# A decoder layer in 16 chunks on one core: new hand-written step orders, a PSUM ring dealt by use, and the weights loaded in two groups

## The chip, the cores and the metric

One Trainium2 chip, of which one core is used. The metric is the device time of one execution in microseconds (us), the median of several runs. Abbreviations: PE is TensorE (PEld its weight loads), DVE is VectorE, ACT is ScalarE, POOL is GpSimd, SP is SyncE, which here only issues DMAs.

## The reference, cut to what matters

All is float32. `x` is 128 sequences of 64 tokens of width 128; `ctx` has the same shape.

```python
# 1. a Mamba block
proj = rms_norm(x) * norm_scale @ in_w + in_b            # 128 -> 512
hidden, gate = split(proj)                               # 256 each
conv = silu(causal_conv4(hidden) + conv_b)
ts, B, C = split(conv @ xproj_w)                         # 64, 16, 16
delta = softplus(ts @ dt_w + dt_b)
for t: state = exp(A * delta) * state + delta * B * conv # 256 channels x 16 states
       y = sum_n(state * C) + D * conv
x = layernorm(x + (y * silu(gate)) @ out_w + out_b)
# 2. cross attention, 16 heads of 8, keys and values from ctx
x = layernorm(x + attention(x, ctx))
# 3. experts: 8 of width 176, top 2 by a router, and one shared
x = layernorm(x + sum_e cw[e] * (silu(x @ wg[e]) * (x @ wu[e])) @ wd[e] + shared(x))
```

## The kernel before, in words

**Chunks and stages.** The batch is cut into 16 chunks of 8 sequences, 512 tokens (`T`). A chunk goes through five stages: *head* (load of x, RMS norm, transposes), *front* (input projections, convolution, B, C, delta), *scan* (16 states, one after the other), *back* (last sums of the scan, output projection, first layer norm, attention, second layer norm, router, start of the experts) and *tail* (rest of the experts, down projection, third layer norm, output).

**Turns.** The program is a sequence of 20 turns, t = -2 to 17. In turn t each engine walks once through a list of its own, `ORDER[engine]`, made from `ORDER_TEXT`. An entry such as `back.up_u3` is a step: stage, name, index. It works on chunk t + `CHUNK_OF[stage]`, with head 2, front 1, scan 0, back -1, tail -2, and is left out where that chunk doesn't exist. So turns 2 to 14 hold all five stages, the first four lack the later stages and the last three lack the earlier ones; all of them use the same lists. Every engine runs its list strictly in order and waits on semaphores inside the steps. A list is a cycle: what stands at its end is followed by what stands at its start, on the next turn.

**Steps that matter below**, on PE unless said otherwise:
- `B_row n` (L478) spreads B of state n over the partitions; DVE `drive n` (L871) multiplies it in PSUM, DVE `scan n` (L881) is the recurrence over [128, 1024]. `B_row n+1` waits for `scan n`, as they share a bank. ACT `decay k` (L630) makes the factors, POOL `prod n` (L1009, and L1014 where two states are joined) multiplies by C, `y_sum k` (L496) adds the product up in PSUM.
- `x1T`, `x2T` (L544) transpose the result of a layer norm. A layer norm is: PE fills a bank (`mout`, `aout`, `down`), DVE `stats` (L855), POOL `stats` (L1027 to L1034), ACT `norm` (L784), which also frees the bank.
- `score`, DVE `score` (maximum, L928), ACT `exp` (8 activations, L760), DVE `sum`, POOL `scale` (L1059), `turn` (L568), ACT `turn` (L769), `mix` (L576), ACT `mix` (L775): attention, eight times per chunk. `aout1` (L582) waits for the last ACT `mix`.
- `up_g i`, `up_u i` (L592), 13 each: gate and up projections of the experts. ACT `up_g` (tanh, L799) and DVE `up_g` (L978) consume a gate bank, DVE `up_u` (L983) or, for i in `ON_POOL`, ACT `up_u` (L807) an up bank. POOL `gu` (L1071) and `cw` (L1080) multiply; the weights of `cw` come over DRAM: PE and ACT `cwT`, SP `cw_out`, SP `cw_in`, two slots. `down` (L608) needs all of them; its first matmul waits for `cw9`, a later one for `cw10`.
- ACT `dt` (L706), `soft` (L712), `soft_ln` (L716, a table load ahead of it and one behind it, ahead of the next tanh or exp), then DVE `delta` (L909, L912): softplus. ACT `squares` (L642) waits for `delta`, since both use `sp_a`.
- POOL `k`, ACT `km`: masked keys. They overwrite what `down` reads and so wait for the last `down1`.

**The ring.** 20 kinds of PE steps (`IN_RING`), 75 steps a turn, write into four PSUM banks. `ring_place` gives a step its bank: the position of the step in the list, modulo 4. A step waits until the bank's user before it has been freed by its consumer (`ring_free`). As 75 is 3 modulo 4, the distance to the user before is 4 steps, but 3 steps for some of the first steps of a turn, and in turns with stages left out the positions that are skipped leave their banks unused.

**The opening.** SP issues 17 weight DMAs (L415), all on the semaphore `weights_in`, and then `x_in` of chunk 0 (L422). PE, ACT, DVE and POOL each wait for all 17. DVE clears `decay`, `hpad`, `vm` and others ahead of that wait and makes 10 more constants behind it, the last but two of them `wu` times 0.5 (L843); PE, ACT and POOL wait for all (`consts_v` at `CONSTS` = 11) before their first step.

Of the kernel before, what the change touches and what calls it, by code (L numbers as in the profile page):

```python
# [73 lines left out]

ORDER_TEXT = {
# [1093 lines left out]
```

## Time and profile before

| | us |
|---|---|
| median of 3 runs | 1959.86 (1947.79 to 1962.64) |
| the profiled execution | 1953.28 |
| its span, first to last instruction | 1951.5 |
| PE busy in it | 1698.4 (87%) |
| POOL busy | 1539.2 (79%) |
| DVE busy | 1508.2 (77%) |
| ACT busy | 1407.5 (72%) |

The 1.8 us between span and time lie before the first and behind the last instruction. A "busy" PE is not one at its peak: its clock is granted at one of two levels, and the same matmul takes twice as long at the lower. Idle time of an engine matters only where the chain that sets the time runs through it.

### The profile page before, as it was taken

How to read it: one execution, taken by the hardware profiler on the slowest of the kernel's cores; microseconds unless marked ns; L12 is line 12 of the kernel's file. 1: busy time of each engine (PE TensorE's matmuls, PEld its weight loads, DVE VectorE, ACT ScalarE, POOL GpSimd, SP SyncE). 2: the span in 40 equal slices, each digit the busy share in tenths (PEclk: the TensorE clock that was granted, in tenths of full speed). 3: DMA queues.
4: the chain of work that ended last, by engine and by line, in shares of the span. 5: the costliest groups of instructions: out<-in, count | busy, mean ns of one | idle time of the engine just before them, and what ended most of it. 6: DMA issues, size and time to landing. Idle time of an engine off the chain costs nothing. (4 is left out here: it accounts for less than half of the span.)

```text
span 1951.5 us, 25799 instructions
## 1 busy us (share of the span) xinstructions
PE 1698.4 (87%) x7138; PEld 975.5 (50%) x7138; DVE 1508.2 (77%) x1891; ACT 1407.5 (72%) x4370; POOL 1539.2 (79%) x1284
## 2 busy tenths in 40 slices
PE   3477898989989899998989999898999989898977
PEld 1124464654646465464646546464655636455644
DVE  3878887887878888788878888788888878878422
ACT  3558778696877968697786869778686967857362
POOL 0457888887878888888888888888888878888735
PEclk8678999999989999999999999899999989999989
DMA  4112131232213223222212322131222312131202
GB/s 123 48 44 66 61 92 54 72 88 85 73 55 88 66 70 88 87 74 74 85 51 68 87 87 83 60 83 60 76 77 87 82 60 77 61 87 60 71 6 65
DMA packets 125918, 140.50 MB, mean 72 GB/s; under 512 B 44048, under 2 KB 69456, under 8 KB 125776
## 3 DMA queue, kind: packets, MB, share of 16 engines
q1 hardware_dynamic: 125776, 138.86, 23.9%
q8 instruction: 58, 0.95, 0.2%
q14 instruction: 84, 0.69, 0.1%
HBM read 133.84 MB, written 4.98 MB: 71 GB/s over the span
## 5 line engine op out<-in xcount | busy, mean ns | idle before, releaser
L1009 POOL TENSOR_TENSOR prod<-state,c_rep 128x1024 f32<-128x1024 f32 x256 | 605.9, 2370 | 43.8 <-DVE state L881 24.0
L881 DVE TENSOR_TENSOR_SCAN state<-decay,p_drive 128x1024 f32<-128x1024 f32 x256 | 583.8, 2280 | 26.8 <-ACT decay L630 14.8
L496 PE MATMUL p_y<-prod,ident 128*128 128x512 f32 x768 | 403.6, 619 | 2.2 <-POOL prod L1014 1.6
L630 ACT ACTIVATE decay<-delta,a_neg 128x504 f32<-128x504 f32 x512 | 361.7, 726 | 60.3 <-DVE state L881 57.1
L871 DVE TENSOR_TENSOR p_drive<-u,p_drive 128x1024 f32<-128x1024 f32 x256 | 312.1, 1219 | 44.1 <-PE p_drive L478 43.6
L760 ACT ACTIVATE ex<-p_ring,nmax 128x64 f32<-128x64 f32 x1024 | 307.8, 355 | 5.4 <-DVE nmax L928 3.1
L592 PE MATMUL p_ring<-x2T,wu 128*128 128x512 f32 x416 | 216.6, 610 | 43.6 <-DVE kT L978 41.9
L592 PE MATMUL p_ring<-x2T,wg 128*128 128x512 f32 x416 | 233.3, 653 | 17.5 <-DVE km L978 10.6
L760 ACT ACTIVATION_READ_ACCUMULATOR ex<-p_ring,nmax 128x1 f32 x1024 | 247.3, 250 | 0.0
L799 ACT ACTIVATE gt<-p_ring 128x512 f32<-128x512 f32 x208 | 123.5, 595 | 102.8 <-PE p_ring L592 102.1
L496 PEld LDWEIGHTS p_y<-prod,ident 128*128 128x128 f32 x768 | 139.7, 197 | 109.5 <-issue 93.9
L1059 POOL TENSOR_TENSOR ex<-ex,rden 128x512 f32<-128x512 f32 x128 | 139.7, 1092 | 65.3 <-DVE rden L932 58.8
L1080 POOL TENSOR_TENSOR km<-km,cwr 128x512 f32<-128x512 f32 x128 | 175.7, 1377 | 8.7 <-DMA cwr<-cw_rows 8.2
L1071 POOL TENSOR_TENSOR km<-km,us 128x512 f32<-128x512 f32 x80 | 115.3, 1442 | 64.3 <-ACT us L807 64.1
L563 PE MATMUL p_ring<-km,qs 128*128 128x512 f32 x256 | 135.7, 613 | 24.0 <-POOL km L1053 18.3
L1014 POOL TENSOR_TENSOR prod<-prod 128x1024 f32<-128x1024 f32 x64 | 150.9, 2357 | 5.0
L592 PEld LDWEIGHTS p_ring<-x2T,wu 128*128 128x128 f32 x416 | 76.9, 194 | 152.9 <-issue 73.1
L576 PEld LDWEIGHTS p_ring<-exT,vm 128*128 128x128 f32 x1024 | 128.9, 191 | 41.0 <-issue 28.7
L592 PEld LDWEIGHTS p_ring<-x2T,wg 128*128 128x128 f32 x416 | 80.4, 205 | 123.6 <-issue 92.1
L576 PE MATMUL p_ring<-exT,vm 128*128 128x128 f32 x1024 | 138.2, 278 | 4.1 <-ACT exT L769 2.2
L784 ACT ACTIVATE x<-p_ring,shift,rstd 128x128 f32<-128x128 f32 x192 | 77.3, 453 | 84.6 <-POOL shift L1034 84.0
L855 DVE BATCH_NORM_STATS2 stats<-p_ring 128x6 f32<-128x128 f32 x192 | 47.1, 287 | 112.7 <-PE p_ring L608 83.9
(138 smaller groups left out, 3171.9 us busy)
## 6 DMA issues: line engine op xcount, KB each, us to landing
c_rep<-c_rows SPq DMA_DIRECT2D x256, 256.0 KB, 3.6
cwr<-cw_rows SPq DMA_DIRECT2D x64, 256.0 KB, 3.2
ctxT<-in_ctx_t SPq DMA_DIRECT2D x32, 256.0 KB, 4.2
cwr<-cw_rows SPq DMA_DIRECT2D x32, 224.0 KB, 2.7
...
```

The costliest lines, as they stand in the source:

```text
L496: pe.matmul(p_y[1 - first][:], ident[:], prod[:, slot_of(c, n), 1 - first, :], start=False, stop=n == STATE - 1).then_inc(prod_used.sem, 1)
L563: mm = pe.matmul(p[:], qs[:, i, :, :].rearrange("p s q -> p (s q)"), km[:, i, :, :].rearrange("p a k -> p (a k)"), start=True, stop=True)
L576: mm = pe.matmul(p[:, 0:128], vm[:, i, q, :], exT[:, q, :], start=q == 0, stop=q == QUADS - 1)
L592: mm = pe.matmul(p[:], (wg if name == "up_g" else wu)[:, i, :], x2T[:], start=True, stop=True)
L630: act.activation(decay[:, n % 2, j, :].rearrange("p (b t) -> p b t", t=SEQ)[:, :, 1:], delta[:, c.parity, j, :].rearrange("p (b t) -> p b ...
L760: e = act.activation(ex[:, i % 2, a, :], p[:, a * SEQ:(a + 1) * SEQ], ACT.Exp, bias=nmax[:, i % 2, a:a + 1], accum_out=den[:, i % 2, a:a + 1])
L871: dve.tensor_tensor(p_drive[:], u[:, c.parity, :, :], p_b.unsqueeze(1).to_broadcast([128, HALVES, T]), ALU.mult).then_inc(drive_ready.sem, 1)
L881: dve.tensor_tensor_scan(state[:, slot_of(c, n), :, :].rearrange("p j t -> p (j t)"), decay[:, n % 2, :, :].rearrange("p j t -> p (j t)"), ...
L1009: pool.tensor_tensor(mine, state[:, slot_of(c, n), :, :], c_rep[:, n % C_SLOTS, :].unsqueeze(1).to_broadcast([128, HALVES, T]), ALU.mult). ...
L1014: pool.tensor_tensor(mine, mine, prod[:, slot_of(c, n - 1), :, :], ALU.add).then_inc(join_ready.sem, 1)
L1059: pool.tensor_tensor(ex[:, i % 2, :, :], ex[:, i % 2, :, :], by_group(rden[:, i % 2, :]).to_broadcast([128, PAIRS, SEQ]), ALU.mult).then_i ...
L1080: pool.tensor_tensor(acts[i], acts[i], cwr[:, slot, :], ALU.mult).then_inc(act_ready.sem, 1)
```

## The change

1. **Three sets of lists.** `FIRST_TEXT` serves turns -2 to 1, `ORDER_TEXT` (new) turns 2 to 14, `LAST_TEXT` turns 15 to 17. All lists hold the same steps as before, but for the place of the cut between two turns: some steps that opened a turn now close the turn before it (on PE 14 steps from `tail.up_g6` to `y_sum29`, now `back.up_g6` and so on; on DVE `drive14` and `scan14`; on POOL `cw7` to `cw9` and `gu10`).
2. **The ring is dealt by use.** The steps that really run, over all turns, get banks 0, 1, 2, 3, 0, ... in turn: the distance is always 4.
3. **Weights in two groups**, behind the first x. `x_in` of chunk 0 comes first, then 9 loads that head and front need (`weights_in`), then 8 others (`weights_late`). PE waits for the late ones at the first `xp`, POOL at the first `add_out_b`, DVE at the first `taps` of chunk 1, where it also scales `wu` (`half_wu`; the first `up_u0` waits for that). ACT and POOL start when only `eps` is there; ACT waits for all constants at its first `hid`. The clearing of `decay`, `vm`, `r_sel`, `r_cw` moves behind the constants on DVE.

```diff
-RING = [step for step in ORDER["pe"] if step[1] in IN_RING]
+USES = [use for t in TURNS for use in steps_at("pe", t) if use[0] in IN_RING]
+PLACE = {use: (k % BANKS, k // BANKS) for k, use in enumerate(USES)}
...
+LAST_FIRST, FIRST_LAST = 1, CHUNKS - 1
+def steps_at(engine, t):
+    part = "first" if t <= LAST_FIRST else "last" if t >= FIRST_LAST else "main"
...
-            for to, src in ((vecs[:], vec), (win[:], w_in), (ident[:], c_ident), (wxp[:], w_xproj),
...
+            sp.dma_start(xf[:], x[bass.ds(0, T), :].rearrange("(g p) d -> p g d", p=128)).then_inc(x_in.sem, 16)
+            for to, src in ((vecs[:], vec), (ident[:], c_ident), (win[:], w_in), (masks[:], c_masks),
+                            (wattn[:], w_attn), (rowb[:, 0, :], rows[0].partition_broadcast(128)),
+                            (rowb[:, 1, :], rows[1].partition_broadcast(128)), (sel_bc32, c_sel_bc),
+                            (less32, c_less)):
                 sp.dma_start(to, src).then_inc(weights_in.sem, 16)
+            for to, src in ((wxp[:], w_xproj), (wdt[:], w_dt), (wout[:], w_out), (wrt[:], w_router),
+                            (tri[:], c_tri), (wg[:], w_gate), (wu[:], w_up), (wd[:], w_down)):
+                sp.dma_start(to, src).then_inc(weights_late.sem, 16)
```

The lists for turns 2 to 14 where the prediction follows them, from the last sums of attention to the first steps that the next turn opened with before ("|" is the cut between two turns):

```
PE before:   back.mix7 back.aout1 scan.y_sum18 back.x2T0 scan.B_row12 back.x2T1 scan.y_sum19 back.route0
             scan.B_row13 front.dt0 back.up_g0 back.up_g1 front.dt1 back.up_u0 back.up_g2 back.up_u1
             scan.y_sum22 scan.B_row14 back.cwT0 back.up_g3 back.up_u2 back.up_g4 front.gate1 back.up_u3
             scan.y_sum23 scan.y_sum26 back.up_u4 scan.B_row15 back.up_g5 back.up_u5 | tail.up_g6
PE after:    back.x2T0 back.mix7 scan.y_sum15 back.aout1 scan.B_row12 front.dt0 scan.y_sum18 scan.y_sum19
             back.x2T1 scan.B_row13 back.route0 front.dt1 back.up_g0 back.up_g1 back.up_g2 scan.B_row14
             scan.y_sum22 back.up_u0 back.up_u1 back.cwT0 back.up_u2 back.up_g3 front.gate1 back.up_g4
             scan.y_sum23 back.up_u3 back.up_u4 scan.y_sum26 scan.B_row15 back.up_g5 back.up_u5 back.up_g6
ACT before:  front.dt0 back.up_g0 back.up_g1 front.dt1 scan.decay29 back.up_g2 front.soft0 scan.decay30
             back.up_u1 back.cwT0 front.soft_ln0 back.up_u2 scan.decay31 back.up_g3 front.gate1 back.up_g4
             head.squares0
ACT after:   front.dt0 back.r_exp0 back.up_g0 scan.decay28 back.up_g1 front.dt1 scan.decay29 back.up_g2
             back.up_u1 scan.decay30 scan.decay31 back.cwT0 front.soft0 back.up_u2 back.up_g3
             front.soft_ln0 back.up_g4 front.gate1 back.up_u4 head.squares0
DVE before:  back.route0 scan.drive13 back.r_rank0 back.up_g0 back.up_g1 scan.scan13 back.r_cw0
             back.up_g2 back.up_u0 | back.drive14 back.scan14 tail.up_g3 scan.delta0 tail.up_u3 tail.up_g4
DVE after:   scan.drive13 back.route0 scan.scan13 back.r_rank0 back.up_g0 back.up_g1 back.r_cw0
             back.up_g2 back.up_u0 scan.drive14 scan.scan14 | tail.up_g3 scan.delta0 tail.up_g4 tail.up_u3
```

Elsewhere in these lists: PE runs `v1`, `B_row4`, `q0`, `y_d0`, `y_d1` between `down1` and `score0` (before: `B_row4`, `q0`, `y_d0`, `v1`); ACT runs `front.tanh1` between `exp3` and `exp4` (before: between `exp1` and `exp2`); DVE runs `drive6` behind `score3` (before: ahead of it); POOL runs `prod12` ahead of `r_rank0` (before: behind it).

## Rows read from the trace of the kernel before

**Rows 1.** Six stretches: busy us by engine (instructions), granted PE clock, DMA share, GB/s.
```profile
0.00:50.40 50.40, 18.55 (x25) 6.27 (x25) 14.81 (x28) 18.78 (x37) 1.20 (x5) 0.83 0.41 123
50.40:129.20 78.80, 46.97 (x78) 16.46 (x78) 65.18 (x43) 39.13 (x69) 45.87 (x20) 0.65 0.16 51
129.20:228.90 99.70, 76.82 (x294) 41.14 (x294) 83.79 (x97) 81.56 (x259) 71.13 (x56) 0.90 0.17 51
228.90:1703.70 1474.80, 1349.67 (x5798) 783.68 (x5798) 1215.09 (x1522) 1138.12 (x3550) 1255.38 (x1041) 0.97 0.25 75
1703.70:1817.70 114.00, 102.06 (x439) 60.11 (x440) 90.12 (x114) 72.18 (x240) 98.27 (x84) 0.97 0.25 77
1817.70:1951.50 133.80, 104.30 (x505) 67.80 (x503) 39.18 (x94) 57.75 (x219) 67.37 (x81) 0.92 0.14 42
```
**Rows 2.** Waits of PE's matmuls, turns 2 to 14: total us, times, longest.
```profile
PE p_ring L592 <- DVE kT L978: 36.4, 13, 3.5
PE p_ring L544 <- ACT x L784: 25.8, 13, 2.0
...
PE p_ring L582 <- ACT aT L775: 8.2, 13, 0.6
```
**Rows 3.** Timeline of PE in one turn: start, us, instructions [idle before <-releaser].
```profile
1001.11 0.41 PE L544 MATMUL p_ring<-ident,x 128*128 128x128 f32 x2 [1.98 <-ACT x L784]
...
1017.51 1.02 PE L592 MATMUL p_ring<-x2T,wg 128*128 128x512 f32 x2
1018.37 1.02 PE L522 MATMUL p_ring<-xnT,win 128*128 128x512 f32 x2
1022.40 1.33 PE L592 MATMUL p_ring<-x2T,wu 128*128 128x512 f32 x2 [3.01 <-DVE kT L978]
```
**Rows 4.** The granted clock around those waits.
```profile
1002.70:1009.50 6.80, 6.80 (x12) 2.37 (x11) 3.58 (x10) 3.14 (x6) 5.01 (x4) 0.50 0.01 2
1023.20:1026.60 3.40, 3.40 (x5) 1.35 (x4) 3.36 (x4) 1.89 (x9) 3.40 (x2) 0.50 0.34 116
```
**Rows 5.** Timeline of ACT between the same two waits.
```profile
1010.71 0.69 ACT L706 ACTIVATE delta<-p_ring,vecs 128x512 f32<-128x512 f32 x1 [0.46 <-PE p_ring L530]
...
1015.85 1.28 ACT L716 ACT_TABLE_LOAD   x1
1017.14 1.06 ACT L716 ACTIVATE sp_a<-sp_a 128x1024 f32<-128x1024 f32 x1
...
1018.71 1.28 ACT L630 ACT_TABLE_LOAD   x1
...
1020.62 0.58 ACT L799 ACTIVATE gt<-p_ring 128x512 f32<-128x512 f32 x1
```
**Rows 6.** Timeline of DVE there.
```profile
1021.66 0.69 DVE L978 SCALAR_TENSOR_TENSOR kT<-gt,p_ring 128x512 f32<-128x512 f32 x1 [2.51 <-ACT gt L799]
1022.26 1.44 DVE L909 TENSOR_TENSOR delta<-delta,sp_a 128x1024 f32<-128x1024 f32 x1
1023.74 2.17 DVE L912 TENSOR_TENSOR u<-delta,h 128x1024 f32<-128x1024 f32 x1
```
**Rows 7.** POOL's longest wait in turns 2 to 14.
```profile
POOL km L1071 <- ACT us L807: 56.5, 13, 7.5
```
**Rows 8.** Groups of POOL in turns 2 to 14: busy us, mean ns of one.
```profile
L1009 POOL TENSOR_TENSOR prod<-state,c_rep 128x1024 f32<-128x1024 f32 x208 | 491.5, 2366 | 13.2 <-DVE state L881 7.9 <-issue 5.0
...
L1080 POOL TENSOR_TENSOR km<-km,cwr 128x512 f32<-128x512 f32 x105 | 145.6, 1392 | 1.6 <-DMA cwr<-cw_rows 1.3
```
**Rows 9.** Timeline of the opening.
```profile
16.04 0.23 ACT L618 ACTIVATE a_neg<-vecs 128x32 f32<-128x32 f32 x1 [14.04 <-DMA rowb<-in_rows]
18.33 0.31 ACT L642 ACTIVATE sp_a<-xf 128x128 f32<-128x128 f32 x1 [2.06 <-DVE a_neg L847]
26.34 0.69 ACT L666 ACTIVATE hpad<-p_ring,vecs 128x512 f32<-128x512 f32 x1 [2.17 <-PE p_ring L522]
```
**Rows 10.** DMA issues of the first 20 us: KB each, us to landing.
```profile
zc<-in_c_less SPq DMA_DIRECT2D x1, 128.0 KB, 2.5
```

More of the change, by code:

```diff
@@ L69 @@
 CHUNK_OF = {"head": 2, "front": 1, "scan": 0, "back": -1, "tail": -2}
+FIRST_TEXT = {
[17 rows of a table added]
+    "act": (
[15 rows of a table added]
+    "dve": (
[12 rows of a table added]
+    "pool": (
[12 rows of a table added]
+}
 ORDER_TEXT = {
     "pe": (
[16 rows of a table removed]
-    "act": (
[15 rows of a table removed]
-    "dve": (
[12 rows of a table removed]
-    "pool": (
[12 rows of a table removed]
[16 rows of a table added]
+    "act": (
[15 rows of a table added]
+    "dve": (
[12 rows of a table added]
+    "pool": (
[12 rows of a table added]
+}
+LAST_TEXT = {
[17 rows of a table added]
+    "act": (
[15 rows of a table added]
+    "dve": (
[12 rows of a table added]
+    "pool": (
[12 rows of a table added]
 }
@@ L142, in read_step @@
     return stage, bare, int(name[len(bare):])
-ORDER = {engine: [read_step(word) for word in text.split()] for engine, text in ORDER_TEXT.items()}
+TEXTS = {"first": FIRST_TEXT, "main": ORDER_TEXT, "last": LAST_TEXT}
+ORDER = {part: {engine: [read_step(word) for word in text.split()] for engine, text in texts.items()}
+         for part, texts in TEXTS.items()}
+TURNS = range(-max(CHUNK_OF.values()), CHUNKS - min(CHUNK_OF.values()))
+LAST_FIRST, FIRST_LAST = 1, CHUNKS - 1
+def steps_at(engine, t):
+    part = "first" if t <= LAST_FIRST else "last" if t >= FIRST_LAST else "main"
+    return [(name, i, t + CHUNK_OF[stage]) for stage, name, i in ORDER[part][engine]
+            if 0 <= t + CHUNK_OF[stage] < CHUNKS]
 IN_RING = ("down", "mout", "k", "xnT", "v", "hid", "x1T", "q", "score", "mix", "turn", "aout",
            "xp", "gate", "x2T", "route", "up_g", "up_u", "cwT", "dt")
-RING = [step for step in ORDER["pe"] if step[1] in IN_RING]
-STAGE_OF = {step[1:]: step[0] for step in RING}
-assert len(STAGE_OF) == len(RING)
+USES = [use for t in TURNS for use in steps_at("pe", t) if use[0] in IN_RING]
+PLACE = {use: (k % BANKS, k // BANKS) for k, use in enumerate(USES)}
+assert len(PLACE) == len(USES)
 class Signal:
@@ L200, in ring_place @@
 def ring_place(name, i, m):
-    stage = STAGE_OF[name, i]
-    at = RING.index((stage, name, i))
-    bank = at % BANKS
-    same = [j for j in range(bank, len(RING), BANKS)]
-    t = m - CHUNK_OF[stage]
-    before = 0
-    for j in same:
-        chunk = t + CHUNK_OF[RING[j][0]]
-        before += min(max(chunk, 0), CHUNKS) + (j < at and 0 <= chunk < CHUNKS)
-    return bank, before
+    return PLACE[name, i, m]
 def build(nc, x, ctx_t, vec, rows, w_in, w_xproj, w_dt, w_out, w_attn, w_router, w_gate, w_up, w_down,
@@ L397, in turns @@
         def turns(engine, step):
-            for t in range(-max(CHUNK_OF.values()), CHUNKS - min(CHUNK_OF.values())):
-                for stage, name, i in ORDER[engine]:
-                    if 0 <= t + CHUNK_OF[stage] < CHUNKS:
-                        step(name, i, Chunk(t + CHUNK_OF[stage]))
+            for t in TURNS:
+                for name, i, m in steps_at(engine, t):
+                    step(name, i, Chunk(m))
         block = stack.enter_context(nc.Block())
@@ L591, in step @@
                 elif name in ("up_g", "up_u"):
+                    if name == "up_u" and c.m == 0 and i == 0:
+                        pe.wait_ge(half_wu.sem, 1)
                     mm = pe.matmul(p[:], (wg if name == "up_g" else wu)[:, i, :], x2T[:],
@@ L660, in step @@
                     act.activation(xnT[:, i * 256:(i + 1) * 256], p[:, 0:256], ACT.Copy,
-                                   scale=column(V_NORM)).then_inc(free(name, i), 1)
+                                   scale=column(V_NORM)).then_inc(free(name, i, c.m), 1)
                 elif name == "hid":
+                    if c.m == 0 and i == 0:
+                        act.wait_ge(consts_v.sem, CONSTS)
                     p = filled(act, name, i, c.m)
@@ L666, in step @@
                     act.activation(hpad[:, i, :, TAPS - 1:], p[:].rearrange("p (b t) -> p b t", t=SEQ),
-                                   ACT.Identity, bias=column(V_INB + i)).then_inc(free(name, i), 1)
+                                   ACT.Identity, bias=column(V_INB + i)).then_inc(free(name, i, c.m), 1)
                 elif name == "tap":
@@ L769, in step @@
                     act.activation(exT[:].rearrange("p a q -> p (a q)"), p[:],
-                                   ACT.Copy).then_inc(free(name, i), 1)
+                                   ACT.Copy).then_inc(free(name, i, c.m), 1)
                 elif name == "mix":
@@ L785, in step @@
                                            scale=rstd[:, ln, g:g + 1], bias=shift[:, ln, g:g + 1])
-                    a.then_inc(free(LN_IN[ln], half), 1)
+                    a.then_inc(free(LN_IN[ln], half, c.m), 1)
                 elif name == "x2T":
                     p = filled(act, name, i, c.m)
-                    act.activation(x2T[:, i * 256:(i + 1) * 256], p[:, 0:256], ACT.Copy).then_inc(free(name, i), 1)
+                    act.activation(x2T[:, i * 256:(i + 1) * 256], p[:, 0:256], ACT.Copy).then_inc(free(name, i, c.m), 1)
                 elif name == "r_exp":
@@ L806, in step @@
                         act.wait_ge(gu_ready.sem, gu_ready.at(c.m - 1, len(ON_POOL) - 2 + k))
-                    act.activation(us[:, k % 2, :], p[:], ACT.Copy).then_inc(free(name, i), 1)
+                    act.activation(us[:, k % 2, :], p[:], ACT.Copy).then_inc(free(name, i, c.m), 1)
                 elif name == "cwT":
@@ L811, in step @@
                         act.wait_ge(cw_out.sem, cw_out.at(c.m - 1))
-                    act.activation(cwT[:], p[0:EXPERTS, :], ACT.Copy).then_inc(free(name, i), 1)
+                    act.activation(cwT[:], p[0:EXPERTS, :], ACT.Copy).then_inc(free(name, i, c.m), 1)
                 elif name == "decay":
@@ L888, in step @@
                 if name == "taps":
+                    if c.m == 1 and i == 0:
+                        dve.wait_ge(weights_late.sem, 16 * n_late)
+                        dve.tensor_scalar(wu[:], wu[:], 0.5, None, ALU.mult).then_inc(half_wu.sem, 1)
                     j, pair = divmod(i, 2)
```

76 lines of the change are left out of this document (38 added, 38 removed), and 220 rows, old and new, of tables (FIRST_TEXT, LAST_TEXT, ORDER_TEXT).

## The prediction

> **What bounds the kernel now.** I read the stretches first. Turns 2 to 14 take 1474.8 of 1951.5 us, 113.4 us each [rows 1]. In them PE is busy 1349.67 us (91.5%), POOL 1255.38 (85%), DVE 82%, ACT 77% [rows 1]. So PE is nearest to being the bound, and what it loses is the first thing to look at: 1474.8 - 1349.67 = 125 us, 9.6 us a turn. The list of its waits names the two largest: a matmul of L592 behind DVE's `kT` (36.4 us, 13 times, 2.8 a turn) and one of L544 behind ACT's norm (25.8 us, 2.0 a turn) [rows 2]. In the timeline these are `up_u3`, which waits 3.0 us for a bank, and `x2T1`, 2.0 us [rows 3]. Each wait is followed by a second loss: right after them the granted clock is 0.50 (1.2 instead of 2.4 GHz) for 6.8 and for 3.4 us [rows 4]. Over all 13 turns the clock is 0.97 [rows 1], so 6% of the time is spent at half rate, 6.8 us a turn, and half of that, 3.4 us, is lost although it counts as busy.
>
> Is PE on the path that sets the time? Followed back from the wait at 1022.40: it is ended by DVE `up_g3` at 1021.66 [rows 6], that by ACT `up_g3` at 1020.62 [rows 5]. ACT ran without a pause from `dt1` at 1010.71 on, with `soft_ln` and its two table loads (1.28 + 1.06 + 1.28 = 3.6 us) in between [rows 5]. `dt1` waited for PE, which came there at half rate from `x2T1` at 1001.11 [rows 3, 4]. `x2T1` waited for the second layer norm. So the loop runs through x2T1, the expert projections, the down projection, attention and the next x2T1, partly on PE and partly on ACT and POOL. The other end stretches are not of that kind: in the first 50.4 us PE is busy 18.55 and DVE 14.81 us, and in the last 133.8 us PE is busy 78%, POOL 50% and the others less [rows 1]. They are bound by latency.
>
> **The opening.** Before, everyone waits for 17 loads: ACT's first operation is at 16.04, and the squares of x start at 18.33, after the constants [rows 9]. After, x and 9 loads (1.1 MB of the 4.1) go first. SP spends some 0.45 us on an issue and 1.3 on the pair for `rowb`; the tenth is issued at about 5.6 us. A load that isn't behind the three large ones lands in 2.5 us (`less` [rows 10]). So the early group is there at 8.1 to 8.5, and ACT starts the squares at about 8.5: 9.8 us sooner. Two covers have to hold. ACT's first `hid` (before at 26.34, after at 16.5 [rows 9]) now waits for constants and for the clears moved behind them: 1.6 us of constants and about 6.6 of clears behind 8.3 end at 16.5, just hidden; if a us late, it costs that us. The first `xp`, a convolution behind that `hid`, waits for the late group, whose bytes are all in by 16 to 17 as before [rows 9]. Value -9.8, between -10.5 and -7.
>
> The Trainium skill ("DMA: Bandwidth & Descriptors", Queues, rings and completion order) states that each of the DMA engines consumes its descriptors in ring order, but that completion is not in order of issue: a small load's semaphore says nothing of an older one on other engines. That speaks for waiting for a count over all nine, as the change does; by it the group is ready at its slowest load. The trace agrees as to the ring order: the small `rowb`, issued last, is what ended the common wait at 16.04 [rows 9].
>
> **Turns 0 and 1** take 78.8 and 99.7 us at clocks of 0.65 and 0.90 [rows 1]. In turn 0 only the scan with front and head run, and its chain B_row, drive, scan can't be shortened: 16 times about 4.4 us is 70. Own lists (no stage that is absent shapes them) can take at most 8 us there; the scaling of `wu` adds 1 us of DVE in turn 0. Value -2.5 for turn 0 and -1.5 for turn 1, together -4, between -12 and +3.
>
> **Turns 2 to 14, wait by wait.** A PE step of 512 columns starts every 0.86 us at full rate [rows 3].
> - `x2T1` (2.0 us). Between `aout1`, which starts its layer norm, and it stood 1.3 us of other PE work; now `dt0`, `y_sum18`, `y_sum19` stand there too, 2.8 us. The latency stays. 1.5 us go.
> - `aout1` (8.2 / 13 = 0.6 us [rows 2]) has `y_sum15` ahead of it now. 0.6 goes, and 0.3 at `aout0` in the same way.
> - `up_u3` (2.8 us). Its bank's user before was `up_g3`, freed by DVE after ACT. Now 4 uses before is `up_u2`, freed by ACT, and `up_g3`'s bank goes to `up_u4`. I count from `x2T1` = 0. PE: `up_g3` starts at 10.4, `up_u4` could at 14.7. ACT, now with `soft_ln` and its loads behind `up_g3` and without waiting for `dt1` at half rate, ends `up_g3` at about 13.7 (before: 20.1 [rows 3, 5]); DVE at 14.6. The 2.8 us go.
> - What comes in their place: `gate1` and `up_g4` are behind `soft_ln` on ACT: 13.7 + 1.28 + 1.06 + 1.28 + 0.6 + 0.7 = 18.6 [rows 5]. `up_g5` takes `gate1`'s bank and could start at 16.7: a new wait of 1.9 us. On DVE `delta0` now has to wait for `soft_ln` at 16.0 and takes 1.44 + 2.17 [rows 6]; `up_g4` follows and frees its bank at 20.3, where `up_u5` could have started at 19.5: 0.8 us. Against these stands the wait of 0.7 that `up_g5` had before. Added 2.0.
> - `score0` waits 1.1 us for POOL's keys. It has 0.9 us more work ahead of it (`y_d1`), but `score1` takes the bank of `down1`, and the norm that frees it comes no sooner: it moves, 0 gained. The wait at `turn0` stays. `drive6` behind `score3` gives ACT its maximum 1.2 us sooner, but ACT is nearly full there, and `tanh1` (0.6) now lies between `exp3` and `turn4`: 0.6 added.
> - POOL: `up_u1` reaches it some 5 us sooner, so its longest wait (4.3 us a turn [rows 7]) shrinks to 2, but then `cw0` waits about 1.3 for its DMA. From `gu1` at 9.5 POOL has up to the end of `cw9` 17 `gu` and `cw` of 1.27 to 1.39 us, `prod13` to `prod15` with a join, 4 x 2.37 [rows 8], and a power of 1.0: 32 to 34 us, with that DMA 43 to 45. PE wants `down0` at 45 by its own work. For a wait of POOL on ACT in between I add 1.0.
> - Clock: the two long waits that the half-rate stretches follow are gone or spread out; I take half of the 3.4 us back, 1.7.
>
> Sum: -(1.5 + 0.9 + 2.8 + 1.7) + (2.0 + 0.6 + 1.0) = -3.3 us a turn, 110.1 us; times 13, -43. Bounds: all of the waits named and all of the clock, nothing added, -8.5; nothing gained and the added waits in full, +3.5.
>
> The ring dealt by use matters little by itself here: the distance was already 4 for all but the first steps of a turn. Dealing costs no instruction. SP's list issues `C13` ahead of `C11` and `C12`, so both wait for `prod9`; they are needed after a join, `prod10` and `stats3`, 6 us later, and land in about 4. Nothing.
>
> **Turn 15 and the end.** Turn 15 has no front, yet takes 114.0 us like the others [rows 1]; POOL is busy 98.27 of them. Its waits are those above, so I take -3.3. In the last 133.8 us the chain is: POOL's `cw` of chunk 14, the down projection, keys, eight rounds of attention, router, projections, `cw` again, `down`. Each step waits for the one before, and the order of independent ones changes little: -1.7. Together -5, between -15 and +4.
>
> **Sum.** -9.8 - 4 - 43 - 5 = -62. The profiled execution took 1953.28 us (span 1951.5), so it would be 1891.5. The median of the three runs is 6.6 us above the profiled one; the same saving from there gives 1898. I take 1895.
>
> **Rivals.**
> 1. *The clock comes back whole.* With no PE wait of 2 us left, the half-rate stretches end, and small waits no longer add up to one: 3.4 instead of 1.7, and a turn without slow stretches reaches `dt1` and `up_u1` sooner, so half of the 3.6 added goes as well. -6.8 a turn, -88: 1953.3 - 88 - 19 = 1846, say 1850. For it: every stretch in rows 4 follows a wait. Against it: the new waits at `up_g5` and `up_u5`. The skill ("TensorE: Matmul & The Clock Gate", A second HAM failure mode: psum-queue depth-cycling) says that micro-idles between groups of matmuls, by cycling through PSUM banks, are enough to make the clock swing. By that rule some of the 3.4 us stays lost; the trace shows falls after waits of 2 and 3 us and can't tell for smaller ones.
> 2. *POOL takes PE's place.* It has 96.6 us of work a turn [rows 1]. If only `gu1`'s wait shrinks and 1.3 us of DMA and 2 us at `gu1` remain, POOL gains 1.1 us a turn: -14 - 19 = -33, 1920. POOL would then be over 87% busy and `down0` would wait for `cw9`.
> 3. *The loop doesn't get shorter*: what goes at `up_u3` comes back at `up_g5`, `up_u5` in full. Then only opening and ends count: -19, 1934 to 1941.
> 4. *Slower.* One mechanism: ACT's queue. `up_g3` stands behind `cwT0`, and that behind the router, whose `r_rank` now follows `scan13` (2.3 us) on DVE. If ACT gets to `cwT0` 5 us later than I count, `up_g3`, `soft_ln`, `gate1`, `delta` and `up_g4` all are 5 us late, PE waits that much more at `up_u4` or `up_g5`, and the clock falls (1.7 more): -3.3 + 5 + 1.7 = +3.4 a turn, +44 - 19 = +25, 1978. It decides from 3.3 us of such delay on for a turn, from about 5 for the whole. Against it: the router has 2 us of spare time in my count.
>
> **How the numbers follow.** Forecast 0.52, rival 1 0.14, rival 2 0.18, rival 3 0.10, rival 4 0.06. The range, 1850 to 1937, reaches from rival 1 to rival 3 and leaves out about 2 in 10. About 1% (20 us) is what a measurement can tell from no change. Faster by over 1%: forecast, rivals 1 and 2, part of 3: 0.86. Within 1%: most of 3: 0.08. Slower: 0.06.
>
> **What would show it.** Squares of x at 8 to 9 us; `hid` at 16 to 17; turns of 109 to 111 us between two `delta`; no wait over 1 us at `x2T1` and `up_u3`, one of about 2 at `up_g5`; clock about 0.98; POOL 87 to 88% busy in turns 2 to 14; the end from the last scan about 130 us. A turn of 113 with new waits on PE would refute the main term, a `hid` at 18 the cover in the opening.

## The result, and the profile after

The kernel after took 1910.16 us (median of 4 runs, 1905.50 to 1915.23), the kernel before beside it 1961.25. The ratio is 0.976, with a 95% interval of 0.973 to 0.979: 2.4% faster. The profiled execution took 1910.89 us, its span is 1909.1 against 1951.5. 1895 had been forecast, 1850 to 1937 as the range. One execution among all those below, the profiled one of t4_drive6, ran about twice as long as the others of its kernel (3382.5 us), and none of its rows is used.

The six stretches of the kernel after (cut at the starts of DVE's `delta0` of chunks 0, 1, 2 and 15 and at the end of its last `gated1`, as in [rows 1]; us, busy us of PE, weight loads, DVE, ACT and POOL, granted clock, DMA share, GB/s):

```profile
0.00:40.20 40.20, 18.51 (x25) 6.26 (x25) 13.99 (x27) 18.59 (x37) 1.20 (x5) 0.79 0.38 122
40.20:114.30 74.10, 44.91 (x75) 15.66 (x76) 65.68 (x44) 38.37 (x68) 45.80 (x20) 0.70 0.23 68
114.30:208.50 94.20, 78.06 (x294) 41.48 (x299) 81.48 (x97) 80.84 (x258) 71.12 (x56) 0.95 0.17 50
208.50:1662.40 1453.90, 1335.90 (x5709) 772.28 (x5800) 1250.56 (x1522) 1129.39 (x3550) 1246.05 (x1041) 0.99 0.25 77
1662.40:1790.50 128.10, 118.65 (x475) 67.02 (x480) 99.10 (x127) 79.92 (x253) 113.96 (x96) 0.97 0.26 82
1790.50:1909.10 118.60, 88.44 (x458) 62.00 (x458) 28.91 (x80) 51.65 (x208) 51.40 (x70) 0.86 0.10 33
```

Set against [rows 1], with the forecast in brackets: opening 50.4 to 40.2, -10.2 (-9.8); turns 0 and 1, 178.5 to 168.3, -10.2 (-4); turns 2 to 14, 113.4 to 111.8 us each, -20.9 in all (-43); turn 15 and the end together, 247.8 to 246.7, -1.1 (-5; the last two stretches only trade 14 us, since the last lists let the scan run later). The sum is -42.4 (-62). So two thirds of the forecast gain came, and what is missing is missing in the main turns. DVE got busier there by 35.5 us although it has the same 1522 instructions [rows 1]; that turned out to be the trail.

PE's busy time in the fourth row is not to be set against [rows 1]: 90 of its matmul records are missing there, all of them of `B_row`, about half of those that ran. Behind a missing record PE looks idle for some 0.3 us longer than it was.

The opening, timeline of ACT (start, us, instruction, idle before and its releaser), answers to [rows 9]:

```profile
8.07 0.23 ACT L754 ACTIVATE a_neg<-vecs 128x32 f32<-128x32 f32 x1 [6.07 <-DMA zc<-in_c_less]
8.21 0.29 ACT L778 ACTIVATE sp_a<-xf 128x128 f32<-128x128 f32 x1
...
16.39 0.69 ACT L804 ACTIVATE hpad<-p_ring,vecs 128x512 f32<-128x512 f32 x1 [2.42 <-DVE r_cw L985]
```

The squares start at 8.21 where 18.33 stood. The first `hid` is at 16.39 and waits for DVE's clears (`r_cw`): that cover is used up, as counted.

The waits of turns 2 to 14 (total us, times, longest) answer to [rows 2, 7]:

```profile
POOL acts_more L1223 <- DMA cwr<-cw_rows: 34.5, 26, 2.9
POOL km L1214 <- ACT us L945: 30.5, 13, 4.2
...
PE p_ring L678 <- ACT x L922: 18.4, 26, 1.0
...
PE p_ring L660 <- DVE h L1041: 13.7, 13, 1.1
...
PE p_ring L728 <- ACT gh L823: 11.8, 12, 1.1
...
PE p_ring L697 <- ACT x L922: 11.0, 13, 0.9
```

`up_u3`'s 2.8 us a turn and `aout1`'s 0.6 are gone, `x2T1` waits 0.45 instead of 2.0 (L678 is `x1T1` and `x2T1` together). POOL's longest wait fell from 4.3 to 2.3 us a turn [rows 7], but its waits for `cwr` rows are now 34.5 us (12.7 before). And PE has new ones: 1.05 us at `front.xp0`, behind DVE's `silu1` (L660), and 0.9 at `up_g5` (L728). Summed up, PE stands idle 9.1 us a turn (1453.90 less 1335.90, over 13), somewhat less for the missing records, where it was 9.6. So the lists took every long wait away and little of the waiting time.

PE where the loop closes, turn 8, answers to [rows 3], and the clock behind it to [rows 4] (PE alone):

```profile
968.84 1.13 PE L710 MATMUL p_ring<-exT,vm 128*128 128x128 f32 x8 [0.40 <-ACT exT L907]
972.24 1.12 PE L664 MATMUL p_ring<-xp_sb,wdt 64*128 64x512 f32 x2 [0.51 <-DVE state L1018]
975.71 0.41 PE L678 MATMUL p_ring<-ident,x 128*128 128x128 f32 x2 [0.43 <-ACT x L922]
...
995.25 1.12 PE L728 MATMUL p_ring<-x2T,wg 128*128 128x512 f32 x2 [1.15 <-ACT gh L823]
996.86 1.12 PE L728 MATMUL p_ring<-x2T,wu 128*128 128x512 f32 x2 [0.49 <-DVE km L1118]
```
```profile
978.90:982.30 3.40, 3.40 (x5) 0.50 0.00 0
```

Half-rate time in turns 2 to 14 fell from 95.6 us to 34.1. Where it is left, it begins 2.2 to 3.7 us behind the start of `x2T1`. The 0.51 ahead of `dt0` in these rows is no wait of `dt0`: the record of `B_row12` is missing there. In s3_drive6_again (below) it is present, and the same place reads

```profile
1064.96 0.39 PE L609 MATMUL p_drive<-xp,sel_bc 128*128 128x512 bf16 x1 [0.19 <-DVE state L1018]
1065.28 1.12 PE L664 MATMUL p_ring<-xp_sb,wdt 64*128 64x512 f32 x2
```

So what stands ahead of the fall is 0.40 at `mix7`, about 0.2 at `B_row12`, 0.43 at `x2T1` and 0.19 at `route0`, and the longest wait before these is `xp0`'s 1.05, 28 us ahead. In s1_d6only (below), where `xp0` doesn't wait, the clock still fell in three turns, one of them at 970.4 us, with no wait over 0.43 in the 30 us before. Rows 3 and 4 had shown it after waits of 2 and 3 us only, and the prediction left open whether it falls without one: it does. That agrees with what the Trainium skill says on micro-idles between groups of matmuls ("TensorE: Matmul & The Clock Gate", A second HAM failure mode: psum-queue depth-cycling). But these small waits don't decide it. They stand at the same places, equal to 0.02 us, in three of the four turns without any half-rate time (in the fourth two of them are longer), and in s3, where no turn has any. What decides stays open.

### The profile page after: what moved, and what is told of

The parts are those of the page before. It is cut to its first block and busy times, and to the rows that moved or that the text cites. A ratio compares the mean times of both kernels' runs of the same rounds, so it can differ in the third digit from the quotient of the medians.

```text
span 1909.1 us, 25699 instructions
## 1 busy us (share of the span) xinstructions
PE 1684.5 (88%) x7035; PEld 964.7 (51%) x7138; DVE 1539.7 (81%) x1891; ACT 1398.8 (73%) x4370; POOL 1529.5 (80%) x1284
## 5 line engine op out<-in xcount | busy, mean ns | idle before, releaser
L627 PE MATMUL p_y<-prod,ident 128*128 128x512 f32 x768 | 391.4, 609 | 10.2 <-POOL prod L1149 5.7
L898 ACT ACTIVATION_READ_ACCUMULATOR ex<-p_ring,nmax 128x1 f32 x1024 | 255.4, 262 | 0.0
L728 PE MATMUL p_ring<-x2T,wg 128*128 128x512 f32 x416 | 226.8, 650 | 13.2 <-ACT gh L823 12.3
L1202 POOL TENSOR_TENSOR ex<-ex,rden 128x512 f32<-128x512 f32 x128 | 144.2, 1127 | 94.1 <-DVE rden L1072 94.1
L728 PE MATMUL p_ring<-x2T,wu 128*128 128x512 f32 x416 | 208.9, 603 | 7.5 <-DVE km L1118 6.5
L1223 POOL TENSOR_TENSOR km<-km,cwr 128x512 f32<-128x512 f32 x128 | 179.6, 1413 | 21.5 <-DMA cwr<-cw_rows 20.3
L697 PE MATMUL p_ring<-km,qs 128*128 128x512 f32 x256 | 135.4, 622 | 25.6 <-ACT x L922 12.7
L728 PEld LDWEIGHTS p_ring<-x2T,wg 128*128 128x128 f32 x416 | 82.3, 205 | 126.2 <-issue 82.9
L710 PEld LDWEIGHTS p_ring<-exT,vm 128*128 128x128 f32 x1024 | 125.0, 191 | 33.1 <-issue 12.0
L744 PE MATMUL p_ring<-wd,km 128*128 128x128 f32 x1024 | 127.9, 279 | 6.9 <-POOL acts_more L1223 6.8
L1214 POOL TENSOR_TENSOR km<-km,us 128x512 f32<-128x512 f32 x80 | 102.6, 1285 | 38.4 <-ACT us L945 37.0
```

The lines of the kernel that those rows point to most:

```text
L627: pe.matmul(p_y[1 - first][:], ident[:], prod[:, slot_of(c, n), 1 - first, :], start=False, stop=n == STATE - 1).then_inc(prod_used.sem, 1)
L710: mm = pe.matmul(p[:, 0:128], vm[:, i, q, :], exT[:, q, :], start=q == 0, stop=q == QUADS - 1)
L728: mm = pe.matmul(p[:], (wg if name == "up_g" else wu)[:, i, :], x2T[:], start=True, stop=True)
L744: mm = pe.matmul(p[:, g * D:(g + 1) * D], acts[j][:, (2 * i + g) * 128:(2 * i + g + 1) * 128], wd[:, j, :], start=False, stop=j == FFN_TIL ...
L898: e = act.activation(ex[:, i % 2, a, :], p[:, a * SEQ:(a + 1) * SEQ], ACT.Exp, bias=nmax[:, i % 2, a:a + 1], accum_out=den[:, i % 2, a:a + 1])
L1202: pool.tensor_tensor(ex[:, i % 2, :, :], ex[:, i % 2, :, :], by_group(rden[:, i % 2, :]).to_broadcast([128, PAIRS, SEQ]), ALU.mult).then_i ...
```

## The experiments

**The change in four parts.** Three kernels build it up from the opening, a fourth leaves out its last lists.

```
# l1_open: opening as changed; before's lists in all turns; before's ring (bank = place in the list % BANKS)
# l2_ring: l1_open with the ring dealt by use
# l3_main: the kernel after with
TEXTS = {"first": ORDER_TEXT, "main": ORDER_TEXT, "last": ORDER_TEXT}
# l4_first: the kernel after with
TEXTS = {"first": FIRST_TEXT, "main": ORDER_TEXT, "last": ORDER_TEXT}
```

> The kernel before with nothing but the opening of the change: x first, weights in two groups, clears behind the constants. Lists and ring as before. Theory 'the opening is carried through': the first delta comes at 40 instead of 50 us, every later turn keeps its length, 10 us less in all, ratio 0.995. Rival 'given back': turn 0 is bound by what it was anyway (the scaling of wu, 1 us, and weights that come late), so that turns 0 and 1 grow by 3 or more and under 7 us are left.

> The kernel above with the ring dealt by use as well; lists still those of before, in all turns. Theory 'the ring by itself does nothing': turns 2 to 14 stay at 113.4 us within 0.3, since the distance was 4 for all but the first few steps of a turn; under 4 us in all. Rival 'the ring is the gain': up_u3 no longer meets up_g3's bank in some turns (as 75 is 3 modulo 4 the dealing shifts the bank but not the distance, so it would have to come from the steps with distance 3), turns shorter by 1 us or more, 13 us in all.

> The change without FIRST_TEXT and LAST_TEXT: the new ORDER_TEXT in all 20 turns. Theory 'each list counts in its own turns': turns 2 to 14 at 111.8 us as in the changed kernel (-1.6 each, -21 in all against the kernel above), turns 0 and 1 near 79 and 100, the whole about 12 us above the changed kernel. Rival 'the new main list does it everywhere': turns 0 and 1 at 74 and 94 already, the whole within 4 us of the changed kernel.

> The change without LAST_TEXT alone: FIRST_TEXT in turns -2 to 1, ORDER_TEXT from 2 on. Theory 'the end is bound by latency, not by order': within 3 us of the changed kernel. Rival 'the last list matters': turn 15 or the end is longer by 5 us or more.

Measured, as ratios to the kernel before: opening 0.994 (0.992 to 0.997), with the ring 0.994 (0.991 to 0.997), with the new main list everywhere 0.986 (0.982 to 0.990), with the first lists too 0.978 (0.974 to 0.982), all 0.976. So the ring by use shows no worth of its own within these intervals, and the other parts add up, but for the last lists, whose share (0.978 to 0.976) the times can't tell from nothing. l3_main lies 17 us above the kernel after where 12 were expected. Row of turns 2 to 14 of l1_open, then turn 0, turn 1 and all from the last `delta0` on of l3_main, then of l4_first:

```profile
218.50:1695.20 1476.70, 1347.94 (x5798) 784.25 (x5798) 1208.66 (x1523) 1139.26 (x3550) 1262.80 (x1041) 0.97 0.25 75
```
```profile
40.30:123.50 83.20, 44.42 (x76) 15.64 (x76) 68.41 (x43) 39.61 (x70) 46.45 (x20) 0.67 0.22 60
123.50:221.90 98.40, 81.33 (x303) 43.26 (x302) 83.72 (x96) 78.19 (x256) 71.62 (x56) 0.93 0.18 49
1675.90:1927.30 251.40, 204.52 (x937) 128.37 (x937) 128.85 (x206) 132.44 (x461) 165.91 (x165) 0.93 0.19 59
```
```profile
38.10:113.80 75.70, 43.62 (x76) 15.32 (x76) 65.87 (x44) 39.16 (x68) 45.58 (x20) 0.70 0.21 66
113.80:207.30 93.50, 78.88 (x299) 41.62 (x299) 81.43 (x96) 80.09 (x258) 71.16 (x56) 0.94 0.18 51
1657.60:1908.10 250.50, 205.08 (x937) 127.77 (x937) 127.50 (x206) 131.99 (x461) 166.20 (x165) 0.94 0.19 59
```

A main turn is 113.6 us with the old list (l1_open) and 111.9 with the new one (l3_main). The new main list is bad in turns 0 and 1 (181.6 us against 178.5 before); the first lists repair that and more (169.2). By the traces the main list also costs some 3 us at the end (250.5 and 251.4 against 247.8), and the last lists win just that back: their gain of about 4 is against the new main list, 1 against the kernel before.

**What bounds the main turns now?** Two kernels take work off POOL and off PE. A third gives the `cwr` rows a third buffer.

```
# t1_pool_less, in POOL's cw
-  pool.tensor_tensor(acts[i], acts[i], cwr[:, slot, :], ALU.mult
+  w = 8 if i in (4, 5) else T
+  pool.tensor_tensor(acts[i][:, 0:w], acts[i][:, 0:w], cwr[:, slot, 0:w], ALU.mult
# t2_pe_less, in PE's y_sum
+  w = 64 if n == 14 else T
+  pe.matmul(p_y[1 - first][:, 0:w], ident[:], prod[:, slot_of(c, n), 1 - first, 0:w], ...
# t3_slots3
-  CW_SLOTS = 2
+  CW_SLOTS = 3
+  cw_slot = [cwr[:, 0, :], cwr[:, 1, :], aT[:]]
```

> The changed kernel, with cw4 and cw5 multiplied over 8 of 512 columns only (leaves out most of the routing weights of these two expert tiles): 2.4 us less of POOL work a turn, between gu1 and cw10. Theory 'POOL bounds the stretch from x2T1 to down1' (61.4 us now, of it 38.3 from gu1 to the end of cw10): turns 2 to 14 fall by 1.5 to 2.4 us from 111.8. Rival 'PE bounds it': no change within 0.4 us.

> The changed kernel, with y_sum28 and y_sum29 over 64 of 512 columns only (leaves out most of state 14 in the sum): 1.5 us less of PE work a turn, in the same stretch from x2T1 to down1. Theory POOL: no change within 0.4 us, PE waits for cw9 or x1T1 instead. Rival PE: turns shorter by 1.2 to 1.5 us, perhaps more by the clock.

> The changed kernel with three slots for the routing weights instead of two (the third is aT, which is idle then): cw_in for cw i no longer waits for cw i-2 but for cw i-3. Theory 'POOL with its DMA waits bounds the stretch': the 3.1 us a turn that POOL waits for cwr (cw8 1.84, cw10 0.74, cw0 0.51) fall to under 1, turns shorter by 1 to 2.5 us, 15 to 35 us in all, which would beat the changed kernel. Rival: the stretch is bound by PE's own work behind it, or SP's queue delays the loads as well: under 0.4 us a turn.

t1 took 1888.1 us (ratio 0.968, 0.960 to 0.976): by the ratios 0.9% less than the kernel after. Its profile shows 1.6 us a turn, of which 1.0 remains between turns without half-rate time (109.6 against 110.6). t2 took 1905.55 (0.977, 0.969 to 0.985), no measurable gain. So PE's own work no longer bounds, and POOL's does in part: rival 2 is half right. t3 didn't do what was expected. POOL's waits for `cwr` rows fell from 44.8 us to 6.3 and POOL ends `cw10` 4.6 us sooner after `x2T1`, yet it took 1916.94 (0.982, 0.976 to 0.989), by the ratios 0.6% more than the kernel after. The two intervals overlap; the traces agree with the times (a main turn is 112.6 us where it was 111.8). The down projection ends 0.7 us later after `x2T1` than in the kernel after: `mout1`, ahead of it on PE, now waits for DVE's `up_u12`.

```profile
PE p_ring L670 <- DVE acts_more L1124: 26.9, 12, 2.3
```

That wait is no second path by the order of the work. The step ahead of `up_u12` on DVE, `gated_h0`, got longer. Its group in turns 2 to 14, in the kernel after and in t3 (busy us, mean ns of one):

```profile
L1045 DVE SCALAR_TENSOR_TENSOR gate<-gate,gh 128x512 f32<-128x512 f32 x26 | 17.8, 683 | 0.0
```
```profile
L1046 DVE SCALAR_TENSOR_TENSOR gate<-gate,gh 128x512 f32<-128x512 f32 x26 | 66.9, 2572 | 0.0
```

In twelve of the thirteen turns `gated_h0` takes 4.8 us instead of 0.7. In t3 POOL's row of `gu` and `cw` has no gap left, and DVE's operation ends when that row does (795.71 to 798.21 are two `cw`):

```profile
793.97 4.78 DVE L1046 SCALAR_TENSOR_TENSOR gate<-gate,gh 128x512 f32<-128x512 f32 x1
```
```profile
794.49 1.27 POOL L1215 TENSOR_TENSOR acts_more<-acts_more,us 128x512 f32<-128x512 f32 x1
795.71 2.50 POOL L1224 TENSOR_TENSOR acts_more<-acts_more,cwr 128x512 f32<-128x512 f32 x2
```

In the remaining one, turn 5 (from 547.1 us on), `gated_h0` takes 1.15, `mout1` doesn't wait, and the turn is 109.15 us long, where turns of the kernel after without half-rate time take 110.2 to 110.9. So where DVE's operation was not held, the third slot went with a turn shorter by over 1 us, as expected; in the other twelve turns the hold cost more than that. That is one turn of one trace; no kernel moved `gated_h0` out of the way.

**Where the main turns lost what they won.** I cut a turn in four legs by the starts and ends of PE's steps (means over chunks 3 to 12, us):

```
                      before   after   s1      s2      s3      s4
x2T1 to end of down1   65.42   61.44   60.86   61.51   60.21   60.67
down1 to score1         6.45    6.29    6.29    6.29    6.29    6.29
score1 to aout0        27.72   29.46   28.20   29.47   28.13   28.13
aout0 to x2T1          13.90   14.64   14.64   14.64   14.62   14.12
```

The first leg won 4.0 us, the attention legs gave 2.5 back (half-rate time lies in the first leg). I suspected the place of `drive6` and `scan6` behind `sum2`, which waits for ACT's `exp2`. t4_drive6 and s3_drive6_again are one kernel, and s1 and s2 are its two halves. One edit in VectorE's main list:

```
 after  "front.silu0 back.score3 back.sum2 scan.drive6 scan.scan6 back.score4 scan.drive7 back.sum3 "
 t4, s3 "front.silu0 scan.drive6 back.score3 back.sum2 scan.scan6 back.score4 back.sum3 scan.drive7 "
 s1     "front.silu0 scan.drive6 back.score3 back.sum2 scan.scan6 back.score4 scan.drive7 back.sum3 "
 s2     "front.silu0 back.score3 back.sum2 scan.drive6 scan.scan6 back.score4 back.sum3 scan.drive7 "
```

> The changed kernel with one local order of DVE put back in the main list: drive6 ahead of score3 and sum2, sum3 ahead of drive7, as it was before. Theory 'DVE's chain of scans in the attention stretch was lengthened by putting drive6 behind sum2, which waits for ACT' (score1 to aout0 29.5 us against 27.7 before): that stretch falls by 0.5 to 1.5 us, turns to about 111. Rival 'the stretch is longer for PE's or ACT's order (tanh1, front.xp0 waiting 1.1 us)': no change or longer.

> The kernel after, and in VectorE's main list only scan.drive6 moved ahead of score3 and sum2 (drive7 stays ahead of sum3). In the kernel after, drive6 and scan6 stand behind sum2, which waits for ScalarE's exp2, so the scan chain stands still for that wait and the later scores of the attention leg come late. Theory (it is this wait that lengthened score1 to aout0 from 27.7 to 29.5 us): that leg is about 28 us, a turn without half-clock stretches about 109.3 us, and the time about 1893 us, some 17 below the kernel after. Rival (it was the order of sum3 and drive7): nothing, 1910 us.

> The kernel after, and in VectorE's main list only sum3 set ahead of drive7 (drive6 stays behind sum2). Theory of drive6's wait: score1 to aout0 stays within 0.3 us of 29.5 and the time is 1905 to 1912 us. Rival: sum3 is what releases ScalarE's scaling of group 3 and TensorE's mix3, so this alone gives the gain: the leg about 28 us and about 1893 us.

> The kernel with both moves in VectorE's main list (the one of t4_drive6) once more, for its trace. Theory: score1 to aout0 about 28 us against 29.5 of the kernel after, turns without half-clock stretches about 109 us against 110.6, half-clock time in turns 2 to 14 no more than the 34 us of the kernel after, span about 1888 us. Rival (the leg is as it was, and the gain is the clock's): half-clock time near 0, turns still 110.5 us.

t4 took 1888.29 us (0.967, 0.961 to 0.974). s3 took 1887.29 (0.966, 0.960 to 0.972), s1 1885.34 (0.964, 0.959 to 0.969), s2 1907.30 (0.975, 0.970 to 0.980). So moving `drive6` alone gives 1.3%, the other half nothing, and the leg is 28.2 us as expected. The leg's 1.26 us a turn are 16 of the 24 us; most of the rest is half-rate time, 13.7 us in turns 2 to 14 of s1 against 34.1. The expected number came, but not for the expected reason. DVE from `drive6` to `silu1` in the kernel after, where `score1` started at 931.64, and POOL beside it:

```profile
940.06 1.21 DVE L1008 TENSOR_TENSOR p_drive<-u,p_drive 128x1024 f32<-128x1024 f32 x1
...
944.94 1.23 DVE L1008 TENSOR_TENSOR p_drive<-u,p_drive 128x1024 f32<-128x1024 f32 x1 [0.71 <-remote]
...
948.46 2.60 DVE L1041 SCALAR_TENSOR_TENSOR h<-h,zc 128x512 f32<-128x512 f32 x1
```
```profile
940.29 1.04 POOL L1202 TENSOR_TENSOR ex<-ex,rden 128x512 f32<-128x512 f32 x1 [0.29 <-DVE rden L1072]
...
947.14 1.05 POOL L1202 TENSOR_TENSOR ex<-ex,rden 128x512 f32<-128x512 f32 x1
948.14 2.37 POOL L1149 TENSOR_TENSOR prod<-state,c_rep 128x1024 f32<-128x1024 f32 x1
```

And the same in s1_d6only, where `score1` started at 924.94:

```profile
938.24 1.23 DVE L1008 TENSOR_TENSOR p_drive<-u,p_drive 128x1024 f32<-128x1024 f32 x1 [1.26 <-PE p_drive L609]
...
941.76 1.08 DVE L1041 SCALAR_TENSOR_TENSOR h<-h,zc 128x512 f32<-128x512 f32 x1
```
```profile
934.39 1.04 POOL L1202 TENSOR_TENSOR ex<-ex,rden 128x512 f32<-128x512 f32 x1 [1.08 <-DVE rden L1072]
...
941.24 1.06 POOL L1202 TENSOR_TENSOR ex<-ex,rden 128x512 f32<-128x512 f32 x1
942.24 2.83 POOL L1149 TENSOR_TENSOR prod<-state,c_rep 128x1024 f32<-128x1024 f32 x1
```

Counted from `score1`, `drive7` starts at 13.30 in both kernels and `silu1` (L1041) at 16.82 in both: the scan chain is no sooner. What differs is that `silu1` takes 2.60 us in the one and 1.08 in the other. In the kernel after POOL's `prod6` has begun 0.32 us before it, and `silu1` ends 0.55 us after `prod6` does. In s1 `silu1` begins 0.48 us before `prod6`, ends 0.54 us after the scaling ahead of it, and now `prod6` takes 2.83 instead of 2.37. The rows read as if each waited for the one that began first. What `drive6`'s move did is this: `sum2` stands 0.8 us later, POOL's scaling of group 2 waits 1.08 for it instead of 0.29, and everything behind it on POOL, `prod6` too, comes 0.8 us later, just behind `silu1`. PE's `xp0`, which waits for `silu1`, stands ahead of `score6`, and so on to `aout0`.

The group of L1041 (L901 before) in turns 2 to 14 says the same without a timeline: busy us, mean ns of one; before, after and s1 in this order (s2 has 50.6, 1946):

```profile
L901 DVE SCALAR_TENSOR_TENSOR h<-h,zc 128x512 f32<-128x512 f32 x26 | 30.6, 1176 | 0.0
```
```profile
L1041 DVE SCALAR_TENSOR_TENSOR h<-h,zc 128x512 f32<-128x512 f32 x26 | 50.6, 1945 | 0.0
```
```profile
L1041 DVE SCALAR_TENSOR_TENSOR h<-h,zc 128x512 f32<-128x512 f32 x26 | 30.6, 1177 | 0.0
```

`silu1` alone takes 0.66 us in chunks 3 to 13 before and in l1_open (there it lies between two products), 2.6 in the kernel after, l3_main, t1, t2, t3 and s2, and 1.1 in s1, s3 and s4. No kernel moved `silu1` alone, so the collision is read from these eleven traces and not tried by itself. The rows agree with the Trainium skill ("SBUF — State Buffer", Who interferes with whom): a DVE instruction with two SBUF inputs contends with a GpSimd instruction that reads SBUF, the port pair they share is an exclusive lock, and the order of issue decides who is blocked. `gated_h0` in t3 shows more than that: it was held through the three POOL instructions that followed the one it met.

The group of L1041 is 20.0 of the 35.5 us by which DVE got busier. Two more groups with two SBUF inputs grew. The six operations a turn of the convolution (`zc<-hpad,halfv,zc`) rose from 71.4 to 86.0 us, and the router's `r_prob` from 2.5 to 14.6; others shrank. `r_prob`, before and after:

```profile
L946 DVE TENSOR_TENSOR r_prob<-r_exp,r_rec 128x32 f32<-128x32 f32 x13 | 2.5, 191 | 0.4
```
```profile
L1086 DVE TENSOR_TENSOR r_prob<-r_exp,r_rec 128x32 f32<-128x32 f32 x13 | 14.6, 1122 | 0.4
```

In turn 8 it runs from 980.69 to 981.79, and POOL's `prod12`, which the new list has ahead of `r_rank0`, from 979.40 to 981.75; before, POOL was idle there. PE's `cwT0` waits 0.98 us for the router in the turns of the kernel after that have no half-rate time, and in every turn of s3; in the kernel before it doesn't wait for it. Whether the turn would be shorter without it was not tried.

**The last leg.** `aout0` to `x2T1` had grown by 0.74 us and no run so far had touched it. The trace of s3 showed POOL's `prod10` waiting for the slot that PE's `y_sum15` frees; the new list has that step behind `mix7`, the old one ahead. `stats3` stands behind `prod10`, and the norm and `x2T1` behind `stats3`.

```
 s3: "... scan.B_row11 back.x2T0 back.mix7 scan.y_sum15 back.aout1 "
 s4: "... scan.B_row11 back.x2T0 scan.y_sum15 back.mix7 back.aout1 "
```

> The kernel of s3_drive6_again, and in TensorE's main list scan.y_sum15 set ahead of mix7, where the kernel before has it. There POOL's prod10 waits 0.7 us a turn for the room that y_sum15 frees, POOL's stats3 stands behind prod10, and norm3 and x2T1 behind stats3: the theory of the second part of the attention leg. It expects prod10's wait and 0.6 to 0.7 us of aout0 to x2T1 (14.62 us, 13.9 in the kernel before) to go, turns of about 108.7 us against 109.3 and a median near 1879 us. Rival (the gain at x2T1 is met by another wait behind it, as with the third slot of t3_slots3, or TensorE's gap falls in a worse place and the clock drops): turns of 109.3 us or more, or half-clock time back, and 1887 us or more.

It took 1876.27 us (6 runs, 1875.19 to 1881.15; ratio 0.9615, 0.957 to 0.966): the fastest of all, by the ratios 1.5% below the kernel after. POOL at that place in s3, then in s4:

```profile
1064.04 2.35 POOL L1149 TENSOR_TENSOR prod<-state,c_rep 128x1024 f32<-128x1024 f32 x1 [0.69 <-PE p_y L627]
1066.36 0.19 POOL L1167 TENSOR_TENSOR var<-mv,eps 128x2 f32<-128x2 f32 x1
```
```profile
1062.87 2.36 POOL L1149 TENSOR_TENSOR prod<-state,c_rep 128x1024 f32<-128x1024 f32 x1
1065.44 0.19 POOL L1167 TENSOR_TENSOR var<-mv,eps 128x2 f32<-128x2 f32 x1 [0.21 <-DVE mv L996]
```

The wait of 0.69 is gone and the leg is 0.50 us shorter, not 0.65, because `stats3` now waits 0.21 for DVE. Of these 0.50 the next leg gives 0.46 back (60.21 to 60.67). Turns without half-rate time go from 109.3 to 109.0 us, 0.3 instead of 0.6: the mechanism held, the rival took half of its worth. Against s3 alone the two intervals overlap, so that this step gains anything by itself is likely, not shown. In the profiled executions of both kernels turns 2 to 14 have no half-rate time at all. Their rows (in the second, 90 records of `B_row` are missing, so its PE time is too low):

```profile
209.00:1630.80 1421.80, 1330.78 (x5799) 767.81 (x5800) 1225.48 (x1522) 1127.93 (x3550) 1250.24 (x1041) 1.00 0.26 79
```
```profile
208.40:1629.20 1420.80, 1315.50 (x5710) 770.20 (x5801) 1216.86 (x1522) 1127.83 (x3551) 1247.02 (x1041) 1.00 0.27 79
```

For s3 that holds for this execution alone. It took 1879.11 us at a mean granted clock of 0.973, and the three others took 1887.00 to 1892.52 at 0.964 to 0.968. The six executions of s4 all lie at 0.971 to 0.974. So of the 11 us between the two medians the reordering's own gain, as the two traces show it, is about 3, and the rest goes along with the clock.

## Why the prediction was right, and where it was not

The time, 1910, lies in the range, 15 us above the forecast; the direction is as forecast. That it came so near is in part luck: sizes missed both ways and partly cancelled. By the four legs the forecast for a main turn was -1.5 from `x2T1` to `down1` (-2.8, -1.7 for the clock, +2.0, +1.0), 0, +0.3 from `score1` to `aout0` (+0.6, -0.3) and -2.1 from `aout0` to `x2T1` (-1.5, -0.6). It came to -4.0, -0.2, +1.7 and +0.7. By its steps:

- **Opening**: right, -10.2 for -9.8, with its start at 8.1 and `hid` at 16.4 as counted.
- **Turns 0 and 1**: undersized, -10.2 for -4. `B_row`, `drive`, `scan` can't be shortened, but turn 0 held 8.8 us beside that chain and lost 4.7 of them. I had taken only a third of the room that I named. Turn 1 lost 5.5 us for 1.5; its half-rate time fell from 20.5 to 10.2 us. Which list entries did that was not tried.
- **`up_u3`, `aout1`, POOL's wait at `gu1`**: right. They are gone, or down to 2.3 us as counted.
- **What comes in their place** at `up_g5` and `up_u5`: 1.4 us for the 2.0 that were added, so a bit better than counted. The leg from `x2T1` to the end of `down1`, where these edits lie, got 4.0 us shorter, 2.5 more than forecast; the excess was not traced.
- **The steps that failed** are the attention part's two: "`tanh1` ... 0.6 added" as its whole price, and the 1.5 and 0.6 that were to go at `x2T1` and `aout1`. The two legs cost 1.74 + 0.74 = 2.5 us, where a gain of 1.8 was forecast. 1.3 of it went when `silu1` no longer stood behind `prod6` (29.46 to 28.20 and 28.13), which I did not price at all: I had looked at what each step waits for by its semaphores, and this wait has none. 0.5 went when `y_sum15` was put ahead of `mix7` again. I had entered that same exchange as a gain (0.6 at `aout1`, which did go from PE's waits), without asking who waits for the slot that `y_sum15` frees. The remaining 0.4 and 0.2 us of the two legs stay open.
- **`x2T1`, "1.5 us go"**: its wait did go from 2.0 to 0.45, but `x2T1` itself came 0.74 us later after `aout0`. A wait that is filled with other work is not by itself a shorter loop.
- **Clock**, 1.7 a turn: right in size, and by itself as large as the whole measured gain of the main list. In the kernel after, the four turns without half-rate time take 110.2 to 110.9 us, the eight with one stretch of 3.4 us 111.6 to 112.6, the one with two 114.0: some 1.6 us for each. Before, turns had 3.4 to 17.1 us of it, 7.4 in the mean, with nearly the same slope (a line through its 13 turns gives 110.4 us + 0.42 for each us at half rate). So 4.7 us less of it a turn is worth about 2, and the waits' own balance was about 0: a turn without half-rate time takes 110.6 us where that line gives 110.4.
- **End**: -1.1 for -5. The order of independent steps gave less than I allowed, and l3 and l4 show that the new main list had made the end 3 us longer first.
- **Rivals**: 2 in part (POOL's work now costs time, PE's doesn't; its 1920 was nearer than the forecast), 3 and 4 not. Against rival 2's own signs, POOL is 86% busy and not over 87, and `down0` hardly waits (2.0 us in 13 turns). Rival 1's mechanism, the clock back whole, came only in one execution of s3 and in s4: no half-rate time, and 1876 us.
- **Signs**: the opening's two came. Turns are 111.8 us, outside the 109 to 111 that were named and short of the 113 that would have refuted the term; `up_g5` waits 0.9 for about 2.
